# Beta added per block, the mask added through TensorE, wide token comparisons, and values two batches behind the logits

## The chip, the cores and the metric

The kernel runs on one core of a Trainium2 chip. The time is device microseconds (us) of one execution; lower is better. PE is TensorE (matrix multiplications and transpositions), DVE is VectorE, ACT is ScalarE, POOL is GpSimd and SP is SyncE, which here only starts transfers. Each engine works through its own list of instructions in order, and semaphores tie the lists together.

## The reference

The input x has 8 batches of 256 rows of 256 numbers; each batch has a context of 77 rows. The reference computes, cut to what matters:

```
x = x + xattn(layernorm(x), ctx, ctx, mask, gamma, beta)
x = x + ffn(layernorm(x), w_gate, w_gate_up, w_down)

xattn: logits = q k^T / 16; logits = -9e15 where mask == 0; attn = softmax(logits)
       h = attn v;  return layernorm_no_affine(h) * gamma + beta
ffn:   probs = softmax(x w_gate) over 8 experts; keep the top 2, divided by their sum
       g, u = x w_gate_up[e];  y_e = (silu(g) * u) w_down[e];  return sum_e probs_e y_e
```

A constant beta is thus part of x after the first line: it goes into the second layer norm, into the gate and into the output.

## The kernel before

The 2048 rows are 16 tiles of 128 rows, two for each batch. The work has four parts.

**Attention loop.** For each batch b, PE transposes x (`turn_x`, L1122), multiplies with the transposed context (`logits`, L1135), transposes the probabilities (`turn_probs`, L1144) and multiplies them with the context rows (`values`, L1160). The context is transposed and put through the gate once for every two batches (`turn_ctx` L1102, `gate_ctx` L1111). PE's loop of round i does `turn_probs(i-1)`, `turn_x(i+1)`, `logits(i)`, a context step, `values(i-1)`. Many small matmuls (`spin`, L1091) are put in ahead of operations so that PE's clock stays up. DVE takes the statistics of x (`x_stats`, L600 to L605), the masked logits with their minimum (`masked_logits`, L617, of the negated logits, with `cap` from the mask), and the scaled values (`scaled_values`, L643). ACT copies the transposed tiles out of PSUM, takes exponents (L938) and squares (L954). POOL turns the mask into `cap` (`caps`, L450), takes powers (`x_rstd` L455, `scales` L467), adds beta to x (`add_beta`, L461) and adds the scaled values (`x1`, L474). SP then writes the rows to `rows_d`, where experts will gather them, and to the output.

**Routing.** Rows are given slots, expert by expert. `choose` (L654 to L662, DVE) finds each row's two experts, in four groups of tiles (4, 4, 6, 2: `GROUPS`). `ranks` (L1173, PE) counts ranks. `slots` (L669 to L682, DVE) makes a slot number and splits it by integer operations into place (low seven bits) and block (high bits). For each tile and each of the two choices there is then a 128x128 one-hot table of places (`place_sel`) and one of blocks times row number (`token_sel`); PE multiplies the pairs (`tokens`, L1186) and so gets a list of rows for each block. `token_sel` is made by DVE, one instruction of 128 columns for each tile and choice (L695, in `select`); `place_sel` by ACT for the first 11 tiles (`BY_ACT`; Abs at L991 for each column block, then a wide Relu at L995) and by DVE for the others (L693). Part of what DVE does for routing stands in the attention loop.

**First block.** The list gives `gather_0`; POOL starts the gather of block 0 (`gather`, L528); DVE takes the row statistics (`row_stats`, L702 to L717); PE transposes (`turn_tok`, L1255) and starts on the gate and up projections (`gate_up`, L1271).

**Experts.** 39 blocks of 128 gathered rows run in a software pipeline: PE does `gate_up` of a block, the transposition of the activations (`turn_act`, L1281) and `down` of the block before (L1291, L1293), with weights split in high and low parts (`split_high` ACT L344, `split_low` DVE L351; the loads are 512 KB pieces through three buffers, a piece starting only when the low part of the piece three before it is done). The result is weighted in two steps, `low_result` (ACT, L1049, the low half of PSUM times the share) and `weighted` (DVE, L831, the high half times the share plus the former), and POOL adds it to the output with an indirect transfer (`add`, L543). POOL's order for each block b is `gather(b+2)`, `add(b-1)`, `row_scale(b+2)`.

## Time and profile before

| what | value |
|---|---|
| median of 3 runs | 469.33 us (467.65 to 470.09) |
| the profiled execution, its own time | 468.22 us |
| its span, first to last instruction | 466.3 us |
| mean granted TensorE clock | 0.964 of full |
| busy: PE, DVE, ACT, POOL | 431.9, 298.0, 225.3, 178.1 us |

The attention loop runs from about 9 to 54 us of the span, routing to about 72 us, the experts' matmuls start at 78 us, are in their steady rhythm from about 98 us and end at 454 us. Each row below says at which microsecond of the span an instruction starts and how long it takes; in square brackets is the idle time of the engine just before it and what ended it.

### The profile page before, as it was taken

How to read it: one execution, taken by the hardware profiler on the slowest of the kernel's cores; microseconds unless marked ns; L12 is line 12 of the kernel's file. 1: busy time of each engine (PE TensorE's matmuls, PEld its weight loads, DVE VectorE, ACT ScalarE, POOL GpSimd, SP SyncE). 2: the span in 40 equal slices, each digit the busy share in tenths (PEclk: the TensorE clock that was granted, in tenths of full speed). 3: DMA queues.
4: the chain of work that ended last, by engine and by line, in shares of the span. 5: the costliest groups of instructions: out<-in, count | busy, mean ns of one | idle time of the engine just before them, and what ended most of it. 6: DMA issues, size and time to landing. Idle time of an engine off the chain costs nothing.

```text
span 466.3 us, 10417 instructions
## 1 busy us (share of the span) xinstructions
PE 431.9 (93%) x2305; PEld 351.0 (75%) x2306; DVE 298.0 (64%) x780; ACT 225.3 (48%) x476; POOL 178.1 (38%) x177
## 2 busy tenths in 40 slices
PE   7688677899999999999999999999999999999980
PEld 4577344778888888888888888888888888888870
DVE  2748898686578457766775457766765477745430
ACT  3485671545465346635644346635643366434330
POOL 5399702233344224423343224423343234422211
PEclk9798778999999999999999999999999999999996
DMA  7633723245255414543542114542542134211121
GB/s 179 224 115 139 230 90 102 71 118 166 69 117 131 114 23 113 124 124 68 146 126 33 34 23 112 126 124 68 141 131 42 25 71 109 34 34 23 13 23 11
DMA packets 29216, 43.90 MB, mean 94 GB/s; under 512 B 3399, under 2 KB 22832, under 8 KB 29200
## 3 DMA queue, kind: packets, MB, share of 16 engines
q1 hardware_dynamic: 19842, 31.94, 22.1%
q0 software_dynamic: 7520, 10.39, 13.6%
q10 hardware_dynamic: 1838, 1.39, 1.2%
q8 instruction: 6, 0.10, 0.1%
q14 instruction: 10, 0.08, 0.1%
HBM read 34.07 MB, written 9.64 MB: 94 GB/s over the span
## 4 chain that ended last, share of the span: by engine, by line
PE 80%; DVE 7%; DMA 3%; POOL 3%; issue 2%; ACT 1%; DVEq 1%; POOLq 0%; ACTq 0%
PE bank L1271 45%; PE bank L1291 15%; PE bank L1293 8%; PE bank L1281 7%; DMA vals<-in_ctx 2%; PE bank L1255 2%; DVE token_sel L695 1%; PE bank L1091 1%; DVE w L351 1%; POOL x_sb L461 1%; DMA out<-y_sb,out_i 1%; POOL att_scale L467 1%; PE bank L1135 1%; DMA tok<-rows_d,gather 1%; POOL x_sb L474 1%
## 5 line engine op out<-in xcount | busy, mean ns | idle before, releaser
L1271 PE MATMUL bank<-w,tokT_hi 128*128 (+1 forms) x624 | 174.2, 401 | 3.0 <-DVE tokT_lo L807 2.1
L543 POOL DMA_INDIRECT out<-y_sb,out_i x39 | 61.7, 1582 | 227.5 <-DVE y_sb L831 227.5
L1271 PEld LDWEIGHTS bank<-w,tokT_hi 128*128 128x128 f32 x624 | 112.9, 190 | 27.2 <-issue 4.9
L1025 ACT ACTIVATE gated<-bank,row_rstd 128x512 f32<-128x512 f32 x78 | 53.6, 688 | 144.0 <-PE bank L1271 144.0
L1291 PE MATMUL bank<-w,aT_hi 128*128 (+1 forms) x312 | 119.5, 418 | 1.0 <-DVE y_sb L831 1.0
L816 DVE SCALAR_TENSOR_TENSOR act<-bank,row_rstd,gated 128x512 f32<-128x512 f32 x78 | 58.5, 749 | 90.3 <-ACT gated L1025 90.3
L1271 PE MATMUL bank<-w,tokT_lo 128*128 (+1 forms) x312 | 97.3, 393 | 0.0
L1293 PE MATMUL bank<-w,aT_lo 128*128 (+1 forms) x312 | 87.6, 281 | 0.0
L1271 PEld LDWEIGHTS bank<-w,tokT_lo 128*128 128x128 f32 x312 | 58.8, 189 | 13.1
L1291 PEld LDWEIGHTS bank<-w,aT_hi 128*128 128x128 f32 x312 | 58.7, 188 | 11.6 <-issue 1.2
L351 DVE TENSOR_TENSOR w<-raw,w (+1 forms) x48 | 58.7, 1262 | 5.9 <-issue 5.8
L1293 PEld LDWEIGHTS bank<-w,aT_lo 128*128 128x128 f32 x312 | 59.1, 189 | 0.0
L822 DVE TENSOR_TENSOR aT_lo<-bank,aT_hi 128x512 fp32r<-128x512 f32 x78 | 53.1, 681 | 0.0
L528 POOL DMA_INDIRECT tok<-rows_d,gather_i x38 | 48.3, 1270 | 9.5 <-issue 6.9
L344 ACT ACTIVATE w<-raw (+1 forms) x48 | 48.4, 1051 | 0.7 <-issue 0.5
L1281 PE MATMUL bank<-ident,act 128*128 128x128 f32 x312 | 46.8, 272 | 0.4 <-DVE act L816 0.4
L1281 PEld LDWEIGHTS bank<-ident,act 128*128 128x128 f32 x312 | 38.8, 141 | 10.8 <-DVE act L816 0.8
L1032 ACT ACTIVATE aT_hi<-bank 128x512 fp32r<-128x512 f32 x78 | 45.9, 589 | 0.3 <-PE bank L1281 0.3
L1091 PE MATMUL bank<-ones 128*128 128x512 bf16 x89 | 31.9, 455 | 13.6 <-ACT vals L912 5.2
L1049 ACT ACTIVATE y_low<-bank,share_at 128x256 f32<-128x256 f32 x39 | 18.5, 475 | 31.3 <-issue 26.7
L536 POOL TENSOR_TENSOR row_rstd<-row_var,neg_half 128x1 f32<-128x1 f32 x39 | 29.5, 757 | 10.8 <-DVE row_var L715 10.8
L831 DVE SCALAR_TENSOR_TENSOR y_sb<-bank,share_at,y_low 128x256 f32<-128x256 f32 x39 | 18.9, 484 | 19.0 <-ACT y_low L1049 15.7
(151 smaller groups left out, 372.6 us busy)
## 6 DMA issues: line engine op xcount, KB each, us to landing
raw<-in_L_ffn_w_gate_up SPq DMA_DIRECT2D x32, 512.0 KB
raw<-in_L_ffn_w_down SPq DMA_DIRECT2D x16, 512.0 KB
rows_d<-x_sb SPq DMA_DIRECT2D x8, 264.0 KB, 2.1
x_sb<-in_x SPq DMA_DIRECT2D x8, 256.0 KB, 8.3
out<-x_sb SPq DMA_DIRECT2D x8, 256.0 KB, 2.6
out<-y_sb,out_i POOLq DMA_INDIRECT x39
tok<-rows_d,gather_i POOLq DMA_INDIRECT x38, 4.2
vals<-in_ctx ACTq DMA_DIRECT2D x1, 462.0 KB
```

Source lines behind the costliest of these rows:

```text
L344: eng.activation(w2[:, bass.ds(c % (2 * PIECES), 1), :, 0, :].rearrange("p a g d -> p (a g) d"), raw[:, bass.ds(c % RAW, 1)].rearrange("p ...
L351: eng.tensor_tensor(piece[:, :, :, 1, :].rearrange("p a g d -> p (a g) d"), raw[:, bass.ds(c % RAW, 1)].rearrange("p a g d -> p (a g) d"), ...
L528: pool.indirect_dma_start(out=tok[:, b % 2, :], out_offset=None, in_=rows_d, in_offset=bass.IndirectOffsetOnAxis(ap=at, axis=0)).then_inc( ...
L543: pool.indirect_dma_start(out=out, out_offset=bass.IndirectOffsetOnAxis(ap=out_i[:, b:b + 1], axis=0), in_=y_sb[:, b % 2, :], in_offset=No ...
L816: dve.scalar_tensor_tensor(out=act[:, h, :], in0=ps_u[h][:, :], scalar=row_rstd[:, s:s + 1], in1=gated[:, h, :], op0=ALU.mult, op1=ALU.mul ...
L822: dve.tensor_tensor(aT_lo[:, h], ps_aT[h][:, :].rearrange("p (k c) -> p k c", k=CH), aT_hi[:, h].bitcast(F32), ALU.subtract).then_inc(aT_l ...
L1025: act_e.activation(gated[:, h, :], ps_g[h][:, :], ACT.Silu, scale=row_rstd[:, s:s + 1]).then_inc(gated_set, 1)
L1032: act_e.activation(aT_hi[:, h], ps_aT[h][:, :].rearrange("p (k c) -> p k c", k=CH), ACT.Copy).then_inc(aT_hi_set, 1)
L1271: ins = pe.matmul(ps[:, :], tokens_[:, s, k, :], w.rearrange("p a g d -> p (a g) d"), start=(k == 0 and tokens_ is tokT_hi and part == 0), ...
L1281: ins = pe.transpose(ps_aT[h][:, c * P:(c + 1) * P], act[:, h, c * P:(c + 1) * P], ident[:])
L1291: pe.matmul(ps_y[:, :], aT_hi[:, h, c, :], w.rearrange("p a t d -> p (a t d)"), start=(h == 0 and c == 0), stop=False, skip_group_check=True)
L1293: ins = pe.matmul(ps_y[:, 0:D], aT_lo[:, h, c, :], w[:, :, 0, :].rearrange("p a d -> p (a d)"), start=False, stop=(h == 1 and c == CH - 1) ...
```

## The change

- **Beta.** x rows are stored without beta. `add_beta` leaves the attention loop. In the experts' part POOL adds beta to each gathered block (128x256) after its gather has landed, ahead of `add(b-1)`; for block 0 DVE does it at the head of `row_stats`. So that the output has its beta, ACT makes share times beta for each block (`share_beta`, 128x256), and `y_low` becomes a DVE instruction (low half times share plus `share_beta`) at the head of `weighted`; ACT's `low_result` is gone. The two shares of a row sum to one.
- **Mask.** DVE makes `ban` (bf16: 0, or -2^119 where masked) in two instructions (308 and 924 columns). PE adds it into the logits by one more matmul with a bf16 identity for each tile. `masked_logits` becomes one maximum over both tiles, the gate's addition and a small product with rstd; ACT's exponent reads PSUM with rstd as its scale. POOL's four `caps` are gone.
- **Slots and tables.** The slot is split in f32 by adding and removing a large constant. `token_sel` is one DVE comparison for a whole group (4 tiles: 1024 columns), of values without the row number; the row number goes into `place_sel`. ACT makes `place_sel` for 12 tiles, Relu by tile with the number as its scale; DVE makes it for the last 4 (12 to 15), two instructions each.
- **Order.** PE's round i is now `turn_x(i+2)`, `values(i-2)`, a context step, `logits(i+1)`, `turn_probs(i)`; ACT's and DVE's rounds follow. Ten rounds instead of nine. The last two values go to banks 0 and 1 and wait for no scaled values. On ACT's queue the second context load and the second mask load are started ahead of the first compute instruction. `select` of group 0 stands inside the loop. The order around block 0 changes: ACT packs the list ahead of `tok_high(0)` and splits pieces 4 and 5 later; DVE makes the block table ahead of `row_stats(0)`, splits piece 4 after `tok_low(1)`, and has `row_stats(1)` ahead of `gate_half(0, 0, 0)`.

```diff
-    BY_ACT = NT - 5
+    BY_ACT = NT - 4
+    MASKED = -2.0 ** 119
+    ROUND = 1.5 * 2.0 ** 30
...
-        ps_att = [bank[i][:, 0:VAL] for i in (4, 5, 6)]
+        ps_att = [bank[i][:, 0:VAL] for i in (4, 5, 6) * 4 + (4, 5, 0, 1)]
...
-            caps(0)
-            x_rstd(0)
-            caps(1)
-            x_rstd(1)
-            pool.wait_ge(beta_in, 16)
-            add_beta(0)
+            for i in range(B // 2 - 1):
+                x_rstd(i)
             scales(0)
...
-            for b in range(2, B):
-                add_beta(b)
+            x_rstd(B // 2 - 1)
+            for b in range(1, B):
                 scales(b)
                 x1(b - 1)
...
+            def add_beta(b):
+
+                pool.wait_ge(beta_in, 16)
+                pool.wait_ge(tok_in[b % 2], arrival(b, b % 2))
+                pool.tensor_tensor(tok[:, b % 2, 0:D], tok[:, b % 2, 0:D], beta_b[:], ALU.add).then_inc(tok_beta, 1)
...
             for b in range(1, NBLK):
                 if b + 2 < NBLK:
                     gather(b + 2, gather_i[:, b + 2:b + 3])
+                    add_beta(b + 2)
                 add(b - 1)
...
+            def bans(i, b0, b1):
+
+                dve.wait_ge(mask_in[i], 16)
+                part = slice(TPB * b0, TPB * b1)
+                dve.tensor_scalar(ban[:, part, :], cap[:, part, :].bitcast(I32), 0.0, MASKED, ALU.is_equal, ALU.mult).then_inc(ban_set, 1)
...
-                for j in range(TPB):
-                    t = TPB * b + j
-                    dve.tensor_tensor_reduce(out=probs[:, b % 2, j, :], in0=ps_logit[b % 2][:, j, 0:T], in1=cap[:, t, :],
-                                             scale=rstd[:, t:t + 1], scalar=-LOWEST, op0=ALU.add, op1=ALU.min,
-                                             accum_out=neg_max[:, t:t + 1]).then_inc(masked, 1)
+                dve.tensor_reduce(most[:, tiles(b)], ps_logit[b % 2][:, :, 0:T], X, ALU.max).then_inc(most_set, 1)
...
+                dve.scalar_tensor_tensor(out=neg_max[:, tiles(b)], in0=most[:, tiles(b)], scalar=-1.0, in1=rstd[:, tiles(b)],
+                                         op0=ALU.mult, op1=ALU.mult).then_inc(masked, 1)
...
+                dve.tensor_tensor(token_sel[:, 2 * g[0]:2 * (g[-1] + 1), :].rearrange("p (n c) q -> p n c q", c=2),
+                                  count_hi[:].unsqueeze(1).unsqueeze(1).to_broadcast([P, n, 2, P]),
+                                  hi[:, part, :].unsqueeze(3).to_broadcast([P, n, 2, P]), ALU.is_equal).then_inc(token_set, 1)
...
             def weighted(b, s):
 
+                dve.wait_ge(share_beta_set, b + 1)
+                dve.wait_ge(down_done, 2 * b + 2)
+                if later(b, 1):
+                    dve.wait_ge(y_set, b)
+                dve.scalar_tensor_tensor(out=y_low[:], in0=ps_y[:, D:2 * D], scalar=share_at[:, s:s + 1], in1=share_beta[:, s, :],
+                                         op0=ALU.mult, op1=ALU.add).then_inc(y_low_set, 1)
...
+                act_e.activation(share_beta[:, s, :], beta_b[:], ACT.Copy, scale=share_at[:, s:s + 1]).then_inc(share_beta_set, 1)
...
+                    ins = pe.matmul(ps_logit[b % 2][:, j, 0:T], ident_b[:], ban[:, TPB * b + j, :], start=False, stop=True,
+                                    skip_group_check=True)
...
+            for i in range(B + 2):
+                g = i // 2 + 1
+                if i + 2 < B:
+                    turn_x(i + 2)
+                if i >= 2:
+                    values(i - 2)
+                if g < PAIRS and i % 2 == 0:
+                    turn_ctx(g)
+                if i + 1 < B:
+                    logits(i + 1)
+                if g < PAIRS and i % 2 == 1:
+                    gate_ctx(g)
+                if i < B:
+                    turn_probs(i)
```

## Rows read from the trace of the kernel before

**Rows 1.** The page: busy time of the engines, and the group of `low_result`.

```profile
PE 431.9 (93%) x2305; PEld 351.0 (75%) x2306; DVE 298.0 (64%) x780; ACT 225.3 (48%) x476; POOL 178.1 (38%) x177
...
L1049 ACT ACTIVATE y_low<-bank,share_at 128x256 f32<-128x256 f32 x39 | 18.5, 475 | 31.3 <-issue 26.7
```

**Rows 2.** Busy time of each engine by stretch of the span, with granted clock.

```profile
20.00:40.00 20.00, 18.31 (x136) 15.18 (x136) 12.51 (x45) 16.02 (x51) 17.26 (x16) 1.00 0.39 128
...
200.00:300.00 100.00, 99.45 (x523) 83.22 (x522) 63.23 (x146) 49.07 (x95) 35.05 (x31) 1.00 0.36 87
```

**Rows 3.** Timeline of POOL in the attention loop.

```profile
25.50 1.27 POOL L461 TENSOR_TENSOR x_sb<-x_sb,beta_b 128x512 f32<-128x512 f32 x1
26.93 0.71 POOL L467 TENSOR_TENSOR att_scale<-att_var,neg_half 128x2 f32<-128x2 f32 x1 [0.16 <-ACT tok L954]
27.61 1.31 POOL L474 TENSOR_TENSOR x_sb<-scaled,x_sb 128x528 f32<-128x528 f32 x1
...
35.76 1.69 POOL L467 TENSOR_TENSOR att_scale<-att_var,neg_half 128x2 f32<-128x2 f32 x1
```

**Rows 4.** Timeline of PE: two transpositions of probabilities, one round apart.

```profile
26.18 0.38 PE L1144 MATMUL bank<-ident,probs 128*77 128x128 f32 x2
...
29.96 0.38 PE L1144 MATMUL bank<-ident,probs 128*77 128x128 f32 x2
```

**Rows 5.** Timeline of DVE: second context sum, masked logits of batches 0 and 7, last scaled values.

```profile
11.39 1.75 DVE L590 TENSOR_REDUCE ctx_sum<-vals 77x6 f32<-77x1536 f32 x1 [1.81 <-DMA vals<-in_ctx]
15.30 0.29 DVE L617 CUSTOM_DVE_ANT_0 probs<-bank,cap,rstd 128x77 f32<-128x77 f32 x1
...
47.81 0.30 DVE L617 CUSTOM_DVE_ANT_0 probs<-bank,cap,rstd 128x77 f32<-128x77 f32 x1 [1.22 <-PE bank L1135]
...
50.59 0.89 DVE L643 SCALAR_TENSOR_TENSOR scaled<-bank,att_scale,gamma_b 128x264 f32<-128x264 f32 x2 [0.59 <-POOL att_scale L467]
```

**Rows 6.** Timeline of DVE: a wide instruction, then routing.

```profile
29.25 1.22 DVE L351 TENSOR_TENSOR w<-raw,w 128x1024 fp32r<-128x1024 f32 x1
...
51.93 1.09 DVE L674 SCALAR_TENSOR_TENSOR slot_i<-both,last_slot 128x4 int32<-128x4 f32 x1
...
53.82 4.51 DVE L695 TENSOR_SCALAR token_sel<-count_to,parts,number 128x128 f16<-128x128 f16 x16 [0.16 <-DVE parts L682]
...
67.17 0.26 DVE L693 TENSOR_SCALAR place_sel<-count_to,parts 128x128 f16<-128x128 f16 x1
...
71.04 0.16 DVE L782 TENSOR_SCALAR count_up<-bank 128x8 int32<-128x8 f32 x1
```

**Rows 7.** Timeline of ACT in routing.

```profile
53.76 4.78 ACT L991 ACTIVATE place_sel<-count_to,parts 128x128 f16<-128x128 f16 x16 [1.26 <-DVEq L685]
58.57 1.91 ACT L995 ACTIVATE place_sel<-place_sel 128x2048 f16<-128x2048 f16 x1
...
64.53 0.84 ACT L995 ACTIVATE place_sel<-place_sel 128x768 f16<-128x768 f16 x1
```

**Rows 8.** Timeline of DVE and PE at block 0.

```profile
75.39 0.43 DVE L702 BATCH_NORM_STATS2 row_stat<-tok 128x6 f32<-128x256 f32 x1 [0.27 <-DMA tok<-rows_d,gather]
...
78.03 2.06 PE L1271 MATMUL bank<-w,tokT_hi 128*128 128x512 f32 x4 [1.08 <-DVE tokT_lo L807]
```

**Rows 9.** Timeline of DVE and PE in block 1.

```profile
92.55 2.36 DVE L351 TENSOR_TENSOR w<-raw,w  x2 [1.69 <-issue]
...
95.63 0.66 PE L1281 MATMUL bank<-ident,act 128*128 128x128 f32 x4 [0.37 <-DVE act L816]
```

**Rows 10.** Steady experts: timeline around one gather, and landing times from 98 to 449 us.

```profile
235.44 1.45 POOL L528 DMA_INDIRECT tok<-rows_d,gather_i  x1 [0.18 <-issue]
...
241.69 0.48 DVE L831 SCALAR_TENSOR_TENSOR y_sb<-bank,share_at,y_low 128x256 f32<-128x256 f32 x1 [0.40 <-ACT y_low L1049]
...
242.51 0.43 DVE L702 BATCH_NORM_STATS2 row_stat<-tok 128x6 f32<-128x256 f32 x1 [0.34 <-issue]
...
245.89 0.38 PE L1255 MATMUL bank<-ident,tok 128*128 128x128 f32 x2
...
DMA to landing us min/median/max: 2.7/4.5/5.3
```

More of the change, by code:

```diff
@@ L113, in build @@
         probs = sb("probs", [P, 2, TPB, T])
+        most = sb("most", [P, NT])
         neg_max = sb("neg_max", [P, NT])
@@ L183, in build @@
         y_low = sb("y_low", [P, D])
+        share_beta = sb("share_beta", [P, 2, D])
         silu_ready = sb("silu_ready", [P, 1])
@@ L681, in slots @@
                 after(route)
-                step(route, dve.tensor_copy(parts[:, :, part, :], parts_i[:, :, part, :]))
-                if 1 <= i < 3:
-                    after(route)
-                    dve.sem_inc(parts_set, 1)
+                dve.scalar_tensor_tensor(out=neg_lo[:, part, :], in0=hi[:, part, :], scalar=-ROUND, in1=slot[:, part, :],
+                                         op0=ALU.add, op1=ALU.subtract).then_inc(parts_set, 1)
             def select(g):
+                n, part = len(g), span(g)
@@ L990, in places @@
                     for c in range(2):
-                        act_e.activation(place_sel[:, 2 * t + c, :], count_to[:], ACT.Abs, bias=parts[:, 0, t, c:c + 1], scale=-1.0
+                        act_e.activation(place_sel(t)[:, c, :], neg_count[:], ACT.Abs, bias=neg_lo[:, t, c:c + 1], scale=-1.0
                                          ).then_inc(apart_set, 1)
-                part = place_sel[:, 2 * g[0]:2 * (g[-1] + 1), :]
-                act_e.wait_ge(apart_set, 2 * (g[-1] + 1))
-                act_e.activation(part, part, ACT.Relu, bias=1.0, scale=-1.0).then_inc(place_set, 1)
-            places(0, range(0, GROUPS[1][-1] + 1))
-            split_high(act_e, RAW)
-            places(1, range(GROUPS[2][0], BY_ACT))
-            for c in range(GU, PIECES):
-                split_high(act_e, c)
+                for t in g:
+                    part = place_sel(t)
+                    act_e.wait_ge(apart_set, 2 * (t + 1))
+                    act_e.activation(part, part, ACT.Relu, bias=number[:, t:t + 1], scale=neg_number[:, t:t + 1]).then_inc(place_set, 1)
+            places(0, GROUPS[0])
+            places(1, GROUPS[1])
+            places(2, range(GROUPS[2][0], BY_ACT))
             act_e.activation(silu_ready[:], neg_half[:, 0:1], ACT.Silu)
+            split_high(act_e, 3)
             act_e.wait_ge(packed_zero, 1)
```

304 lines of the change are left out of this document (147 added, 157 removed).

## The prediction

> **What bounds the kernel now.** I read the page first: PE is busy 93% of the span and no other engine over 64% [rows 1]. That is an average over unlike stages, so next came the busy time by stretch. From 200 to 300 us PE works 99.45 of 100 us [rows 2]: whatever DVE, ACT or POOL gain or lose in the experts costs nothing until it makes PE wait. From 20 to 40 us POOL is busy 17.3, PE 18.3 and ACT 16.0 of 20 us: three engines are nearly full, and a gain on one meets the next soon. The timelines and the chain of waits then show the stages:
>
> - Start and attention loop. DVE sums the large context load when it has landed, at 11.39, and only then come the first masked logits, at 15.30; those of batch 7 stand at 47.81 and the scaled values of batch 6 at 50.59 to 51.48 [rows 5]. That is (47.81 - 15.30) / 7 = 4.64 us a batch. In it POOL pays beta 1.27, power 0.71 and addition 1.31 [rows 3], and its power takes 1.69 at 35.76. PE's round is 29.96 - 26.18 = 3.78 us with no gap [rows 4].
> - Routing. From 51.48 to 71.04 DVE works without a pause that counts; the list needs its last table [rows 6].
> - First block: the gathered rows are read at 75.39 and PE starts at 78.03 [rows 8].
> - Then PE is the bound to the end.
>
> So the change can pay only ahead of 78 us, and can lose anywhere.
>
> **Attention loop, part by part.** POOL loses eight beta additions (1.27 each) and the mask's work; what stays is 0.71 + 1.31 = 2.0 us a batch, so POOL is no bound. DVE takes over the mask: by the wide row, 1.22 us for 1024 columns [rows 6], 924 columns cost about 1.1 and 308 about 0.5. Nothing in the trace has this form (int32 in, bf16 out); half and double that price are the ends, 0.8 and 3.2 for both. PE adds 16 bf16 matmuls of 77 columns. No row has one; the two 128-column transpositions of rows 4 together take 0.38 including their drain, so I take 0.1 each, with ends of 0 and 0.25. A full round is then 3.78 + 0.2 = 4.0 us on PE.
>
> *Start.* In the old order the masked logits of batch 0 wait on DVE behind the sum of six contexts (1.75) and a second set of statistics. In the new one they stand behind a sum of two and the small mask part, and the load is asked for earlier. I take 12.7 for 15.3. The ends are 11.5 (load no matter) and 15.3 (both early loads delay the x rows by as much).
>
> *Rounds.* Round 0 ends when the first exponents are done, 12.7 + 0.9 = 13.6. Round 1 needs the second mask part, which DVE makes behind the sum of four contexts: 17.5. Rounds 2 to 5 are full ones at 4.0: 33.6. Rounds 6 and 7 have no x to turn, but DVE chooses experts in them: I take 3.2 each, an estimate between half of a full round and a full one, so 40.0. Then the values of batch 6 (about 1.3), a square (0.5) and the power (0.71 plus a hop, 0.8) give 42.6. DVE is still at the first wide comparison, to 43.2, and ends the scaled values 0.9 later, at **44.1 against 51.5: a gain of 7.3**. If the rounds keep the old 4.64 from round 2 on, the end is 3.9 later (4 x 0.64 + 2 x 0.64); if the start gives nothing either, 6.5 later: gain 0.8. The other end is 1.2 earlier plus cheap bans, a gain of 9.
>
> **Routing.** Old, from the scaled values' end: 71.04 - 51.48 = 19.6 us on DVE. New: slots(1) 1.05 (six small steps where there were eight), select(1) 1.22, choose 1.9, last gates and scaled values 1.2, slots(2) 1.1, choose 1.1, the last addition 0.6, select(2) of 1536 columns 1.8, slots(3) 1.0, places 4 x 0.23 = 0.9, select(3) 0.7, places 0.9: 13.4. **Gain 6.2**; most is select, where 16 narrow instructions of 0.28 (4.51 [rows 6]) become two of 1.22, one of them inside the loop, and 20 such steps behind the last slots (from 67.17) become one wide one and eight narrow, select(2) going ahead of them. The wide comparison (f32 in, f16 out) has no row; its ends are 1.0 and 2.0 us for each 1024 columns: -0.8 or +2.4 on the sum.
>
> What is next late is ACT. It makes places for 12 tiles: two Abs of 0.30 (4.78 / 16) and one Relu of 256 columns. From 1.91 for 2048 and 0.84 for 768 columns [rows 7] the Relu is 0.84 ns a column and 0.2 fixed, 0.4 us, or 0.35 when pipelined: 0.95 a tile, 11.4 us in all. ACT begins about where the old one did against the scaled values, 1 us after them, and ends at 12.4, just ahead of DVE's 13.4. But PE holds tokens(1), which needs eight tiles (8.6), ahead of ranks(3), and slots(3) on DVE (due at 9.8) needs that. So the cover is about 1 us; gone, each us of ACT costs one.
>
> One rule speaks against my sum. At 51.93 a small DVE instruction with two inputs takes 1.09 us [rows 6] while POOL is in an addition, and the power at 35.76 takes 1.69 instead of 0.71 [rows 3]. The Trainium skill (SBUF — State Buffer, section Who interferes with whom) says that a DVE instruction with two SBUF inputs and a GpSimd instruction that reads SBUF exclude each other for the whole instruction; these rows agree. By that rule the wide comparisons of groups 0 and 1, which now have two SBUF inputs, can each wait out one `x1` of POOL, and the gain would be some 2.6 us less. My range has that in it.
>
> **First block and ramp.** DVE adds beta to block 0 on the path: by the 1.27 for 512 columns on POOL at most 0.7, by the wide DVE row (1.22 for 1024) 0.4; with a hop **+0.45**. The block table leaves the spot ahead of `tok_low(0)` and two index steps enter: **-0.1**. In block 0 DVE now splits piece 4 behind `tok_low(1)` (1.2); part of it meets idle time, but in block 1 the split at 92.55 already runs so late that PE waits 0.37 at 95.63 [rows 9]: **+0.8**, with ends 0 and 3 (piece 7's load may start only when piece 4 is split, and a late load would hold ACT).
>
> **Steady experts.** For each block ACT gives up 0.475 [rows 1] and takes share_beta, about 0.4; DVE takes 0.48 more, in 9.4 us of which a third is idle [rows 2]. POOL adds beta, about 0.65 (half of 1.27). All this lies beside PE. What could break the cover is the new wait: behind `add_beta` on POOL are the indirect addition and the row power, and DVE's row statistics wait for it. The gather starts at 235.44, lands 2.7 to 5.3 us later (median 4.5), and the statistics start at 242.51, 7.07 after it [rows 10]. Even 5.3 + 0.65 + 0.1 = 6.05 is inside; PE needs the result for 245.89, and the statistics take 1.3 of these 3.4 us, which is 2 us more cover. y_low on DVE instead of ACT takes the same 0.48, but now behind `act_low`: 0.15 later, with the last block alone paying. **+0.15**.
>
> **The sum.** -7.3 - 6.2 + 0.45 - 0.1 + 0.8 + 0.15 = -12.2. The profiled execution took 468.22 us: 456.0. The median of the runs is 469.33, 1.1 above it: 457.1 in their terms, which I give as 457.
>
> **The rivals.**
>
> 1. *The loop hardly gains.* ACT's or DVE's queue, each in order and with more rounds in flight, sets 4.64 again, and the early loads only trade places. For it: three engines over 80% busy [rows 2]. Against: POOL is the fullest without a gap from its beta on, and PE's own round is 3.78. Only 0.8 to 3 of the 7.3 come: -6 or so, 463.
> 2. *ACT's places bound routing.* If a tile costs 1.2 instead of 0.95, ACT ends 3 us later and slots(3) waits: -9, 460.
> 3. *The gather's new wait stalls PE, and the kernel is slower.* Place: `add_beta` on POOL, then row statistics, then `turn_tok`. It decides when landing plus beta exceeds 7.07 + 2 = 9.1 us after the start of the gather. At 9.6 it costs 0.5 us in each of 37 blocks, 18.5: 469.3 - 12.2 + 18.5 = 475.6. Against: 6.05 is the worst that the rows give.
> 4. *No change.* The wide comparison takes 2.0 and more, the loop gains nothing, and the ramp takes 3: about 468.
>
> **Chances.** Forecast (453 to 461.5, with rival 2 inside it at 0.12): 0.70. Rival 1: 0.18. Rival 3: 0.06. Rival 4: 0.06. A measurement of this kernel tells about 0.5% (2.3 us) from no change. Faster: 0.70 + 0.17 = 0.87, same 0.06, slower 0.07. The range takes in the forecast and most of rival 1: 452.5 to 464.5.
>
> **What would show it.** Right: scaled values of batch 6 end near 44 and PE's full rounds take 4.0 to 4.3; `token_sel` is four instructions, the 1024-column ones near 1.2; `count_up` starts near 57.5; PE's first `gate_up` near 65; in the experts POOL's beta addition is about 0.65 and ends over 1 us ahead of the statistics, and PE stays above 99% busy. Wrong: DVE's row statistics waiting on POOL with PE idle at `turn_tok`; `ranks` of the last group waiting on ACT's places; PE at half clock through the loop; the masks' load landing late, so that logits of batch 2 wait for `ban`; or a hole around blocks 0 and 1, with ACT held by piece 7.

## The result: slower, and the profile after

The changed kernel takes 472.45 us (median of 5 runs, 472.24 to 473.82) against 469.33 (467.65 to 470.09): ratio 1.0094, with a 95% interval of 1.0070 to 1.0117. The quotient of the two medians alone is 1.0066. Either way the kernel is slower, by about 1% and by less than 2%; ratios below are those on record. The forecast was 457, so sign and range are both wrong. The profiled execution of the changed kernel has a span of 470.3 us, that of the kernel before 466.3; the stages below are cut from these two.

| stage (us of span) | before | forecast | after | after, three orders mended |
|---|---|---|---|---|
| to the first masked logits or maxima | 15.30 | 12.7 | 16.94 | 11.84 |
| loop, to the end of batch 6's scaled values | 36.18 | 31.4 | 41.00 | 35.28 |
| routing, to `count_up` | 19.56 | 13.4 | 14.36 | 14.04 |
| first block, to PE's first `gate_up` | 6.99 | 7.3 | 9.12 | 7.57 |
| ramp, to `gate_up` of block 2 | 19.72 | 20.5 | 19.88 | 19.96 |
| experts, to the end | 368.55 | 368.7 | 369.00 | 369.31 |
| span | 466.3 | 454.1 | 470.3 | 458.0 |

Routing gave 5.2 of the 6.2 us foreseen. The start lost 1.6, the loop 4.8 and the first block 2.1. The last column is the experiment `e6_three` below.

The page of the changed kernel: busy time of the engines, the new beta addition, and the spin matmuls of PE with what they waited for.

```profile
PE 431.9 (92%) x2318; PEld 352.6 (75%) x2319; DVE 310.1 (66%) x770; ACT 225.0 (48%) x488; POOL 189.4 (40%) x206
...
L533 POOL TENSOR_TENSOR tok<-tok,beta_b 128x256 f32<-128x256 f32 x38 | 28.2, 743 | 110.0 <-DMA tok<-rows_d,gather_i 110.0
...
L1106 PE MATMUL bank<-ones 128*128 128x512 bf16 x86 | 30.0, 442 | 14.4 <-DVE scaled L651 7.1
```

PE's busy sum is that of [rows 1] to the tenth, so the kernel did not get slower by more PE work: it waits more. The third row says for whom: of the 14.4 us of waiting ahead of the spin matmuls, half is for DVE's scaled values. Next, the busy time by stretch (us busy of PE, PE's loads, DVE, ACT, POOL, then the granted clock, DMA share, GB/s; the DMA share is the profile's own figure and comes out a little over 1 in places).

```profile
8.00:12.00 4.00, 0.17 (x3) 0.02 (x1) 0.00 (x0) 0.86 (x2) 0.08 (x1) 1.00 0.89 242
12.00:16.00 4.00, 3.58 (x23) 3.58 (x23) 3.07 (x15) 1.10 (x4) 0.73 (x1) 0.62 1.09 382
16.00:20.00 4.00, 4.00 (x22) 3.54 (x21) 2.35 (x6) 2.10 (x5) 0.32 (x1) 0.53 0.21 64
20.00:40.00 20.00, 16.91 (x131) 13.98 (x130) 13.39 (x50) 15.43 (x45) 7.66 (x8) 1.00 0.32 105
200.00:300.00 100.00, 99.46 (x523) 83.31 (x522) 68.45 (x155) 46.60 (x96) 43.55 (x42) 1.00 0.35 84
```

From 20 to 40 us POOL fell from 17.26 to 7.66 us busy, as the change was to do, and PE fell too, from 18.31 to 16.91 [rows 2]: every engine has idle time, PE 15% of the stretch, and yet the loop is slower. Such a stage is not bound by an engine but by a ring of waits. From 8 to 12 us next to nothing works: ACT 0.86 us, PE 0.17, DVE none.

**Start.** DVE's timeline (start, duration, line, operation, in square brackets the idle time and its releaser), then the row of the chain of waits.

```profile
7.45 0.17 DVE L744 SCALAR_TENSOR_TENSOR wg_sb<-bank,w_gate_sb 128x16 f32<-128x16 f32 x1 [2.93 <-PE bank L1214]
12.11 0.18 DVE L748 SCALAR_TENSOR_TENSOR wg_sb<-wg_sb,gamma_c 128x16 f32<-128x16 f32 x1 [4.48 <-DMA beta_c<-in_L_xattn_beta]
...
16.94 0.32 DVE L623 TENSOR_REDUCE most<-bank 128x2 f32<-128x154 f32 x1 [1.70 <-PE bank L1153]
```

```profile
3.69 8.32 DMA beta_c<-in_L_xattn_beta
```

A load of 0.5 KB takes 8.32 us; by then ACT has asked for the large loads of context, mask and gamma (issued from 1.46 to 3.45 us), and `e1_loads` below shows that these are the reason. The median of such small loads is 5.4 us for gamma's and 6.8 for beta's columns, where it was 2.6 and 2.4 before. DVE waits 4.48 us for the last one, PE behind DVE, and PE's granted clock is then 0.62 and 0.53 in the mean of the next two stretches, mostly its lower level (1.2 GHz). The kernel before has the same dip, with PE waiting for the contexts:

```profile
12.00:16.00 4.00, 1.12 (x5) 0.70 (x5) 3.93 (x18) 1.41 (x4) 1.08 (x1) 0.65 1.10 356
16.00:20.00 4.00, 3.49 (x17) 3.23 (x17) 1.66 (x9) 1.43 (x4) 2.46 (x3) 0.50 0.37 135
```

So the clock is no loss against the kernel before; it is a gain that a quicker start can still collect.

**Loop.** One round on DVE, POOL and PE.

```profile
34.46 0.88 DVE L651 SCALAR_TENSOR_TENSOR scaled<-bank,att_scale,gamma_b 128x264 f32<-128x264 f32 x2
37.54 0.32 DVE L623 TENSOR_REDUCE most<-bank 128x2 f32<-128x154 f32 x1 [2.20 <-PE bank L1153]
...
37.89 0.54 DVE L629 SCALAR_TENSOR_TENSOR neg_max<-most,rstd 128x2 f32<-128x2 f32 x1
38.35 1.21 DVE L366 TENSOR_TENSOR w<-raw,w 128x1024 fp32r<-128x1024 f32 x1
39.49 0.88 DVE L651 SCALAR_TENSOR_TENSOR scaled<-bank,att_scale,gamma_b 128x264 f32<-128x264 f32 x2
```

```profile
37.10 1.31 POOL L478 TENSOR_TENSOR x_sb<-scaled,x_sb 128x528 f32<-128x528 f32 x1
41.45 0.71 POOL L472 TENSOR_TENSOR att_scale<-att_var,neg_half 128x2 f32<-128x2 f32 x1 [3.04 <-ACT tok L972]
42.13 1.30 POOL L478 TENSOR_TENSOR x_sb<-scaled,x_sb 128x528 f32<-128x528 f32 x1
```

```profile
40.03 0.39 PE L1106 MATMUL bank<-ones 128*128 128x512 bf16 x1 [0.95 <-DVE scaled L651]
```

The ring can be read off: `x1` on POOL from 37.10 to 38.41 (1.31); `neg_max`, 0.16 us of work (it takes that in the first four batches), ends only with it, and the split behind it brings DVE to 39.49 (1.08); the first of the two scaled values frees PE's bank at 40.03 (0.54); PE's values, ACT's square and the hops bring POOL to its power at 41.45 (1.42); the power to the next `x1` at 42.13 (0.68). The sum is 5.03 us, and around the three rounds in which DVE splits weights the scaled values start at 29.43, 34.46, 39.49 and 44.51, 5.03 apart. The round forecast was 4.0, the old one 4.64. A second way round lies beside this one and is not much shorter: scaled values, PE's logits, the maxima (42.08), `neg_max`, the split, the next scaled values. `e12_half_x1` shows what is left when POOL no longer sets the time: 4.5 to 4.65.

**Routing.** DVE's timeline, and POOL's beside it.

```profile
55.17 1.22 DVE L693 TENSOR_TENSOR token_sel<-count_hi,hi 128x1024 f16<-128x1024 f32 x1
57.05 0.89 DVE L651 SCALAR_TENSOR_TENSOR scaled<-bank,att_scale,gamma_b 128x264 f32<-128x264 f32 x2 [0.65 <-POOL att_scale L472]
...
58.87 2.38 DVE L693 TENSOR_TENSOR token_sel<-count_hi,hi 128x1024 f16<-128x1024 f32 x1
...
68.95 0.17 DVE L677 TENSOR_TENSOR slot_c<-bank,chosen 128x16 f32<-128x16 f32 x1 [0.37 <-PE bank L1193]
...
72.30 0.16 DVE L793 TENSOR_SCALAR count_up<-bank 128x8 int32<-128x8 f32 x1
```

```profile
55.61 1.35 POOL L472 TENSOR_TENSOR att_scale<-att_var,neg_half 128x2 f32<-128x2 f32 x1 [1.07 <-ACT tok L972]
...
58.87 1.29 POOL L478 TENSOR_TENSOR x_sb<-scaled,x_sb 128x528 f32<-128x528 f32 x1
```

The wide comparison costs 1.22 us, as taken. The second starts in the same moment as an `x1` and takes 2.38: it ends 1.09 us after that `x1`, nearly as if it had begun only then. The first in turn stretches POOL's power from 0.71 to 1.35. In the profile of `e6_three` below, the second comparison went first: it took 1.22, but `x1` took 2.37 and DVE's next step waited 1.19 for it. Which of the two goes first does not matter here; the 1.2 us are lost either way.

```profile
48.06 2.37 POOL L478 TENSOR_TENSOR x_sb<-scaled,x_sb 128x528 f32<-128x528 f32 x1
```

```profile
50.47 0.56 DVE L662 TENSOR_TENSOR versus<-x_sb 128x384 f32<-128x384 f32 x1 [1.19 <-POOL x_sb L478]
```

**First block.** DVE, then ACT, then PE.

```profile
76.81 0.42 DVE L711 TENSOR_TENSOR tok<-tok,beta_b 128x256 f32<-128x256 f32 x1 [0.49 <-DMA tok<-rows_d,gather]
77.27 0.43 DVE L713 BATCH_NORM_STATS2 row_stat<-tok 128x6 f32<-128x256 f32 x1
...
80.55 0.25 DVE L869 TENSOR_SCALAR spare_at<-packed,spare_no 128x39 f32<-128x39 f32 x1 [2.04 <-ACT packed L1034]
...
80.95 0.42 DVE L817 TENSOR_TENSOR tokT_lo<-bank,tokT_hi 128x256 fp32r<-128x256 f32 x1
```

```profile
78.25 0.18 ACT L1034 ACTIVATE packed<-bank 128x16 f32 x1 [4.80 <-issue]
78.84 1.68 ACT L1034 ACTIVATE packed<-bank 128x16 f32 x6 [0.41 <-ACT packed L1034]
80.42 0.38 ACT L1038 ACTIVATE tokT_hi<-bank 128x256 fp32r<-128x256 f32 x1
```

```profile
81.42 0.80 PE L1294 MATMUL bank<-w,tokT_hi 128*128 128x512 f32 x1 [2.60 <-DVE tokT_lo L817]
```

From the row statistics to `gate_up` it took 75.39 to 78.03, 2.64 us, before [rows 8]; now 77.27 to 81.42, 4.15 us. The seven packing copies now stand ahead of `tokT_hi` on ACT, and DVE's index steps, which need them, ahead of `tokT_lo`. The first of the copies starts only at 78.25 because ACT first reads seven start values into registers (seven loads at L1029, starting from 74.2 to 77.6 us). The other 0.6 us of this stage's loss lie ahead of the statistics, most of them the beta addition (0.42 and a hop).

**Experts.** One gather with its beta addition on POOL, and the statistics on DVE.

```profile
239.24 1.45 POOL L525 DMA_INDIRECT tok<-rows_d,gather_i  x1 [0.18 <-issue]
244.41 0.72 POOL L533 TENSOR_TENSOR tok<-tok,beta_b 128x256 f32<-128x256 f32 x1 [3.72 <-DMA tok<-rows_d,gather_i]
```

```profile
246.35 0.43 DVE L713 BATCH_NORM_STATS2 row_stat<-tok 128x6 f32<-128x256 f32 x1 [0.33 <-issue]
```

The addition ends at 245.13, 1.2 us ahead of the statistics, which do not wait for it. PE is busy 99.46 of the 100 us from 200 to 300.

### The profile page after: what moved, and what is told of

Same layout as the page of the kernel before. It is cut to its first block, busy times and chain, and to the rows that moved or that the text cites. A ratio compares the mean times of both kernels' runs of the same rounds, so it can differ in the third digit from the quotient of the medians.

```text
span 470.3 us, 10470 instructions
## 1 busy us (share of the span) xinstructions
PE 431.9 (92%) x2318; PEld 352.6 (75%) x2319; DVE 310.1 (66%) x770; ACT 225.0 (48%) x488; POOL 189.4 (40%) x206
## 4 chain that ended last, share of the span: by engine, by line
PE 81%; issue 5%; DVE 5%; POOL 3%; DMA 3%; ACTq 1%; SPq 1%; DVEq 0%; ACT 0%; POOLq 0%
PE bank L1294 46%; PE bank L1314 15%; PE bank L1316 8%; PE bank L1304 7%; DMA beta_c<-in_L_xattn_beta 2%; PE bank L1278 2%; POOL x_sb L478 1%; PE bank L1106 1%; PE bank L1151 1%; POOL att_scale L472 1%; DMA out<-y_sb,out_i 1%; DVE w L366 1%; ACTq L1029 1%; DVE token_sel L693 1%; PE bank L1137 1%
## 5 line engine op out<-in xcount | busy, mean ns | idle before, releaser
L533 POOL TENSOR_TENSOR tok<-tok,beta_b 128x256 f32<-128x256 f32 x38 | 28.2, 743 | 110.0 <-DMA tok<-rows_d,gather_i 110.0
L1314 PEld LDWEIGHTS bank<-w,aT_hi 128*128 128x128 f32 x312 | 58.7, 188 | 12.1 <-issue 1.3
L366 DVE TENSOR_TENSOR w<-raw,w (+1 forms) x48 | 56.8, 1220 | 5.8 <-issue 5.6
L1304 PEld LDWEIGHTS bank<-ident,act 128*128 128x128 f32 x312 | 38.9, 141 | 11.5 <-DVE act L826 1.6
L1106 PE MATMUL bank<-ones 128*128 128x512 bf16 x86 | 30.0, 442 | 14.4 <-DVE scaled L651 7.1
L1106 PEld LDWEIGHTS bank<-ones 128*128 128x128 bf16 x86 | 8.5, 107 | 24.6 <-DVE scaled L651 9.5
```

Source lines behind the costliest of these rows:

```text
L366: eng.tensor_tensor(piece[:, :, :, 1, :].rearrange("p a g d -> p (a g) d"), raw[:, bass.ds(c % RAW, 1)].rearrange("p a g d -> p (a g) d"), ...
L1304: ins = pe.transpose(ps_aT[h][:, c * P:(c + 1) * P], act[:, h, c * P:(c + 1) * P], ident[:])
L1314: pe.matmul(ps_y[:, :], aT_hi[:, h, c, :], w.rearrange("p a t d -> p (a t d)"), start=(h == 0 and c == 0), stop=False, skip_group_check=True)
```

## The experiments

Each ratio is to the kernel before, run on the same chip in the same session; "the changed kernel" is at 1.0094. Times in us from different sessions differ by up to 0.4% for one kernel (the kernel before had medians of 467.68 to 469.47), so the ratios are what to compare. Stages and rounds are from one profiled execution of each run.

### e1_loads: the large loads go back to where they stood

```diff
-            act_e.dma_start(vals[:, 2:B, 1:D + 1], ctx_t[:, 2:B, :])...
...
-            act_e.dma_start(cap[:, 4:NT, :]..., mask_t[:, 2:B, :])...
-            act_e.dma_start(gamma_b[:, 0:D], ...)...
             centre(0)
             centre(1)
+            act_e.dma_start(vals[:, 2:B, 1:D + 1], ctx_t[:, 2:B, :])...
+            act_e.dma_start(cap[:, 4:NT, :]..., mask_t[:, 2:B, :])...
+            act_e.dma_start(gamma_b[:, 0:D], ...)...
...
-            ctx_means(1, 2, 4)
             bans(0, 0, 2)
             x_stats(0)
+            ctx_means(1, 2, 4)
```

> The changed kernel with the second context load, the second mask load and gamma's load started after the first two centring steps again, and DVE's sum of contexts 2 and 3 behind the first statistics. Theory A (the four small column loads on SP's queue land late, at 12.0 us, because the early large loads keep the DMA engines busy): the last column load lands before 8 us, the first maximum of the logits starts at 12 to 13.5 instead of 16.94, and the end comes 3 to 4.5 us earlier: 468 to 469.5 against 472.5. Rival B (the columns are late for another reason, or the x rows only trade places with the contexts): under 1 us. The rounds of the attention loop keep their 5.03 us by both.

467.47 us (465.20 to 469.76), ratio 0.9980 (0.9960 to 1.0000): the early loads cost some 5 us, 1.1% of the kernel. The edit also moves one DVE sum (`ctx_means`, 0.8 us) back behind the statistics; what that alone gives was not measured. The stretch 8:12 and DVE's first maxima in this kernel:

```profile
8.00:12.00 4.00, 3.07 (x31) 2.76 (x30) 3.14 (x17) 1.28 (x4) 1.05 (x1) 1.00 1.09 273
```

```profile
11.54 0.30 DVE L623 TENSOR_REDUCE most<-bank 128x2 f32<-128x154 f32 x1
```

The small columns land in 2.3 to 2.5 us again (medians), which is Theory A. The first maxima are 5.4 us earlier, and the clock stays at 1.00 to 28 us. The execution profiled took 465.20 us, 2.3 less than the median, so the full clock through the start is shown for it and not for the others. The rounds of the loop are still 5.03 (scaled values at 23.53, 28.56, 33.59, 38.61). Start and loop are two separate losses.

### e9_cols_first: the small columns ahead, the large loads still early

```diff
-            load_x(0)
             sp.dma_start(w_gate_sb[:], ...)
...
+            load_x(0)
```

> The changed kernel with one thing moved: SyncE issues the gate matrix and the four column loads of gamma and beta (0.5 KB each) ahead of the load of x of batch 0; the early large loads of ctx and mask stay where the change put them. Theory (it is the small columns that come late, because they are asked for while the large loads are moving): they land before 8 us instead of at 12.0, x of batch 0 about 3 us later than in the changed kernel, and the first maxima start at 13 to 14.5 instead of 16.94; the rounds stay at 5.03, and the time is 2.5 to 4 us below the changed kernel, 468.5 to 470. Rival (the early large loads hold everything, whatever the order of the small ones): the columns or x of batch 0 still land near 12, first maxima at 16 or later, time within 1 us of the changed kernel's 472.4.

474.63 us (472.05 to 475.72), ratio 1.0117 (1.0066 to 1.0168): no gain where 2.5 to 4 us were expected; the theory fell, the rival held. DVE's timeline, and the stretch 8:12:

```profile
9.94 0.18 DVE L748 SCALAR_TENSOR_TENSOR wg_sb<-wg_sb,gamma_c 128x16 f32<-128x16 f32 x1 [2.07 <-DMA beta_c<-in_L_xattn_beta]
...
12.18 0.75 DVE L613 BATCH_NORM_STATS2 stats<-x_sb 128x6 f32<-128x256 f32 x2 [0.96 <-DMA x_sb<-in_x]
```

```profile
8.00:12.00 4.00, 0.00 (x0) 0.00 (x0) 1.24 (x5) 0.00 (x0) 0.30 (x1) 0.77 1.03 339
```

The columns come 2.2 us earlier and x of batch 0 now lands at 12.1 (8.92 us after its issue in the chain of waits). Whatever stands behind is late: the cause is not the order of the small loads but that 1.05 MB of context, mask and gamma (462, 462 and 128 KB) share the DMA engines, some 90% busy from 4 us on, with what the first batch needs. First maxima: 18.52.

### e2_split_first: DVE's split and choice ahead of the next batch's maxima

```diff
+                if 3 <= i < 6:
+                    split_low(dve, i - 3)
+                if i == 6:
+                    choose(GROUPS[0])
                 if i + 1 < B:
                     masked_logits(i + 1)
                 if i < 3:
                     x_stats(i + 1)
-                if 3 <= i < 6:
-                    split_low(dve, i - 3)
-                if i == 6:
-                    choose(GROUPS[0])
```

> The changed kernel with DVE's weight splits and choose of group 0 put ahead of the masked logits of the same round. Theory A (a ring of waits sets the round: scaled values free a bank, PE does the second values, context step and logits, 2.1 us; DVE's maximum and small product, up to 1.5; then the split, 1.2, stands ahead of the next scaled values, 0.5): the split then lies beside PE's part, a round falls from 5.03 to 3.8 to 4.2 us, and five rounds give 4 to 6 us: 467 to 468.5. Rival B (ACT, POOL or the number of batches in flight sets the round): it stays near 5.0 and the time within 1 us of 472.5.

467.96 us (465.68 to 472.29), ratio 0.9981 (0.9957 to 1.0005). Scaled values start at 32.46, 36.35, 40.81, 44.86, 48.75: rounds of 3.9 to 4.5 in place of 5.03 and 5.4. `neg_max` still takes 1.01 to 1.18 us in each of them, but no split stands between the end of `x1` and the scaled values any more.

### e3_logits_first: PE's context and logits ahead of the values

```diff
-                if i >= 2:
-                    values(i - 2)
                 if g < PAIRS and i % 2 == 0:
                     turn_ctx(g)
                 if i + 1 < B:
                     logits(i + 1)
+                if i >= 2:
+                    values(i - 2)
```

> The changed kernel with PE's context step and logits(i+1) ahead of values(i-2), nothing else. Theory A (the ring): the logits no longer wait behind the values that wait for a bank, so DVE gets its maximum about 1.5 us earlier in a round, and the ring loses PE's logits: rounds of 4.0 to 4.4 instead of 5.03, 3 to 5 us in all: 467.5 to 469.5. Rival B (something else sets the round): no change, or slower, since the values come later and with them squares and powers.

470.62 us, ratio 1.0044 (1.0010 to 1.0077): a gain of 0.5%, where the order on DVE gives 1.1%, and less than the 3 to 5 us expected. Rounds 5.6, 4.75, 4.86, 4.0, and `neg_max` takes 0.16 us in all of them: it no longer meets `x1`, and DVE's scaled values wait about 1 us for POOL's power in its place. The maxima come sooner, but the values, which POOL's power waits for, come later: this shortens one way round the ring and lengthens the other.

### e10_negmax: `neg_max` with one tensor operand

```diff
-                dve.scalar_tensor_tensor(out=neg_max[:, tiles(b)], in0=most[:, tiles(b)], scalar=-1.0, in1=rstd[:, tiles(b)], ...)
+                for t in range(TPB * b, TPB * (b + 1)):
+                    ins = dve.tensor_scalar(neg_max[:, t:t + 1], most[:, t:t + 1], rstd[:, t:t + 1], -1.0, ALU.mult, ALU.mult)
```

> The changed kernel with neg_max made by two DVE instructions for one column each (one tensor operand from SBUF, the scale as a per-row scalar) instead of one with two tensor operands from SBUF. Theory: the one instruction takes 1.01 us where it does 0.16 us of work since it waits for POOL's addition x1; two of the new kind take 0.2 to 0.4 together even beside x1, and since neg_max is a link of the ring that sets the round, the round falls from 5.03 to 4.2 to 4.5 us, scaled values of batch 6 end 3 to 4 us earlier against the first maxima, and the time is 469 to 470. Rival (DVE instructions wait for POOL whatever their operands, or the ring isn't what sets the round): neg_max's group still takes about 1 us or the rounds stay at 5.0, time 472 to 473.

476.30 us (472.20 to 476.94, four runs), ratio 1.0142 (1.0080 to 1.0204). The expectation was wrong on the time and on the round: it falls to 4.95, not to 4.2 to 4.5. DVE and POOL of one round:

```profile
41.18 0.33 DVE L630 TENSOR_SCALAR neg_max<-most,rstd 128x1 f32<-128x1 f32 x2
41.43 1.35 DVE L366 TENSOR_TENSOR w<-raw,w 128x1024 fp32r<-128x1024 f32 x1
...
42.71 0.88 DVE L652 SCALAR_TENSOR_TENSOR scaled<-bank,att_scale,gamma_b 128x264 f32<-128x264 f32 x2
```

```profile
40.39 1.31 POOL L478 TENSOR_TENSOR x_sb<-scaled,x_sb 128x528 f32<-128x528 f32 x1
```

`neg_max` no longer waits (0.203 to 0.215 us in all 16), but the split behind it, which also reads two tensors, does: it ends 1.08 us after `x1`'s end at 41.70, and the splits of the rounds before and after, which took 1.82 and 1.83 us, also end 1.08 us after the end of their `x1`. Until this run I had taken the ring for one of PE and DVE alone with `neg_max` as a slow link; it goes through POOL. That the kernel was slower than the changed one lies in the start of this profile: PE had half clock from 12 to 24 us, and the first scaled values start at 32.80 for 29.43. The edit touches nothing before the first maxima, so why the start was slower stays open.

### e12_half_x1: a shorter addition on POOL

```diff
-                pool.tensor_tensor(x_sb[:, tiles(b), :], scaled[:, b % 2], x_sb[:, tiles(b), :], ALU.add)
+                pool.tensor_tensor(x_sb[:, tiles(b), P:], scaled[:, b % 2, :, P:], x_sb[:, tiles(b), P:], ALU.add)
```

> The changed kernel with POOL's addition x1 over the upper 136 of 264 columns only; it leaves out the attention's part of columns 0 to 127 of the result. Theory (a second ring goes through POOL: x1 holds off DVE's next two-operand instruction, neg_max or the split; the split then delays the scaled values, these PE's values, these ACT's square, and that the power and the next x1): with x1 at about 0.67 us instead of 1.31 neither neg_max nor the split waits for it, and the round is what the PE ring leaves without a wait, about 0.35 from PE's logits to neg_max's start, 0.12, 1.15 for the split: 4.65 to 4.75 us instead of 5.03, three rounds, 1 us in all. Rival (the ring is PE and DVE alone and takes 5.03 with or without POOL): rounds of 5.0 to 5.05, and neg_max or the split still longer than 0.16 and 1.21 us.

The addition leaves out the attention's part of columns 0 to 127. 470.07 us, ratio 1.0048 (1.0025 to 1.0072), by the ratios 2.2 us below the changed kernel. Rounds of 4.47, 4.65 and 4.49. DVE and POOL:

```profile
39.46 0.16 DVE L629 SCALAR_TENSOR_TENSOR neg_max<-most,rstd 128x2 f32<-128x2 f32 x1
39.54 1.22 DVE L366 TENSOR_TENSOR w<-raw,w 128x1024 fp32r<-128x1024 f32 x1
40.67 0.88 DVE L651 SCALAR_TENSOR_TENSOR scaled<-bank,att_scale,gamma_b 128x264 f32<-128x264 f32 x2
```

```profile
38.67 0.76 POOL L478 TENSOR_TENSOR x_sb<-scaled,x_sb 128x272 f32<-128x272 f32 x1
```

Here `x1` ends at 39.43, ahead of `neg_max`, and both DVE instructions have their own length; that round is 4.65, PE's and DVE's share alone. In the two others (no context to transpose, so the maxima come sooner) `neg_max` still waits a little, 0.46 us. So of the 1.03 us by which the changed kernel's round exceeds the forecast 4.0, at least 0.4 to 0.55 are the wait for POOL's addition, on an engine that is busy 38% of that stretch, and the rest is the second way round, with the split between the maxima and the scaled values.

### e4_pack and e5_block0_order: the first block

`e4_pack` moves `tok_high(0, 0)` on ACT and `tok_low(0, 0)` on DVE back ahead of the packing and the index steps:

```diff
+            tok_high(0, 0)
             for e in range(1, E):
                 pack(e)
-            tok_high(0, 0)
```

> The changed kernel with ACT's copy of the turned rows of block 0 and DVE's low part ahead of the packing of the list again, as in the kernel before. Theory A (ACT's reading of seven start values, which ends at 78.25, and then seven packing steps, 2.2 us, stand in front of block 0's transposed rows): PE's first gate_up starts 1.6 to 2.4 us earlier against the start of the gather, and the time falls by 1.5 to 2.3: 470 to 471. Rival B (the later gather list of block 1 takes it back: its rows then come later, as in the kernel before): PE's first gate_up is earlier but block 1 starts later, under 0.7 us in all.

473.52 us (471.82 to 474.28), ratio 1.0108 (1.0071 to 1.0145): no gain. Statistics to `gate_up` fell from 4.15 to 2.48 us, as expected of the cause, but the next transposition of rows then waited 1.65 us for DVE and the `gate_up` behind it 0.74; `count_up` to `gate_up` of block 2 took 29.35 us against 29.00. The rival held: an early first block runs into a late second one.

`e5_block0_order` also puts `block_experts`, the splits of pieces 4 and 5 (DVE's and ACT's) and `gate_half(0)` back where the kernel before had them (DVE's part shown):

```diff
-            block_experts()
             split_low(dve, 3)
+            split_low(dve, 4)
             row_stats(0, 0, 0)
+            block_experts()
...
-            row_stats(1, 1, expert_of(1))
             gate_half(0, 0, 0)
+            row_stats(1, 1, expert_of(1))
```

> The changed kernel with the whole order around block 0 put back: ACT copies the turned rows before it packs, DVE does two splits before the first row statistics and the block table after them, and row statistics of block 1 after the first half of the activations; ACT's splits 3 to 5 stand ahead of the packing. Theory A (packing in front costs 1.7 at the first gate_up, and e4 lost it again because the statistics of block 1, which wait for a late gather, stood ahead of the activations): from count_up to the first gate_up of block 2 it takes 27 to 27.7 us instead of 29.0, time 1.3 to 2 us below the changed kernel's: 470.5 to 471. Rival B (ACT's three splits after the place tables now delay the packing, or PE's clock falls in the wait): no gain.

471.39 us, ratio 1.0051 (1.0030 to 1.0072). `count_up` to `gate_up` 7.57 us, and to that of block 2 27.79 against 29.00 (26.71 in the kernel before). So the loss was in the order of the whole stretch, not in the packing alone.

### e7_beta_only and e8_wide_only: each idea without the rest

`e7_beta_only` is the kernel before with beta added for each block and through `share_beta`; `e8_wide_only` the kernel before with wide `token_sel` comparisons and the row number moved into the place tables. Neither has the new orders.

```diff
-                add_beta(b)
...
                     gather(b + 2, gather_i[:, b + 2:b + 3])
+                    add_beta(b + 2)
...
-                        dve.tensor_scalar(token_sel[:, 2 * t + c, :], count_to[:], parts[:, 1, t, c:c + 1], number[:, t:t + 1], ...)
+                dve.tensor_tensor(token_sel[...n tiles...], count_f[:]..., parts[:, 1, part, :]..., ALU.is_equal)
```

> The kernel before with only the beta part of the change: stored rows have no beta, POOL adds it to each gathered block, DVE to block 0, ACT makes share times beta, DVE makes y_low. Theory A (hidden beside PE in the experts; in the loop POOL was nearly full, so it gains some there): loop 2 to 4 us shorter, first block 0.45 later, experts equal within 0.5: 466 to 468. Rival B (the gather's new wait on POOL or DVE's extra 0.48 makes PE wait in the experts): 470 or more. Rival C (the loop is bound by the others too): within 1 us of before.

468.43 us, ratio 0.9993 (0.9968 to 1.0019). The loop gains 2.7 us (14.57 to 48.09), the first blocks give back 1.0 and the experts took 1.5 more than in the profile of before (PE busy 99.05 of the 100 us from 200 to 300, for 99.45). With that nothing is left that can be measured, as rival C had it for the total, although the loop did gain.

> The kernel before with only the wide comparisons: token_sel by one comparison for a group, the row number in the place tables, slots as before with integers, DVE still makes the places of the last 5 tiles. Theory A (16 narrow instructions of 0.28 become two of 1.22, and 20 later steps become one wide one and ten narrow): count_up 3.5 to 5 us earlier, 464.5 to 466. Rival B (ACT's Relu by tile takes more than the one wide Relu and bounds): 1 to 2 us only.

467.62 us, ratio 0.9960 (0.9940 to 0.9981): faster by 0.4%, less than expected. Routing took 17.3 us for 19.56, a gain of 2.3 where 3.5 to 5 were expected. The first two comparisons took 3.41 us together, for 2 x 1.22, one of them beside an addition on POOL, and PE waited 1.17 us for ACT's places, so both the exclusion between DVE and POOL and rival 2 of the prediction show here a little.

### e6_three: the change with three orders mended

`e1_loads`, `e2_split_first` and `e5_block0_order` together; no arithmetic differs from the changed kernel.

> The changed kernel with three repairs: the loads of e1, the split ahead of the masked logits of e2, the order around block 0 of e5. Theory A (three separate losses that add up: 5.3 and 5.3 by the runs of e1 and e2, about 1.5 by e5): 12 us below the changed kernel, about 460 to 461, ratio to the kernel before 0.981 to 0.985. Rival B (the gains of e1 and e2 are largely one, the clock of PE in the first 25 us): 464 to 466.

459.46 us (459.10 to 459.93), ratio 0.9793 (0.9756 to 0.9830): faster than both kernels, and 3.0% below the changed kernel, where the gains of `e1_loads`, `e2_split_first` and `e5_block0_order` (1.1, 1.1 and 0.4%) add up to 2.7%. Its DVE timeline:

```profile
11.84 0.30 DVE L623 TENSOR_REDUCE most<-bank 128x2 f32<-128x154 f32 x1
...
26.44 1.01 DVE L629 SCALAR_TENSOR_TENSOR neg_max<-most,rstd 128x2 f32<-128x2 f32 x1
27.37 0.88 DVE L651 SCALAR_TENSOR_TENSOR scaled<-bank,att_scale,gamma_b 128x264 f32<-128x264 f32 x2
```

The stages are in the table above. `neg_max` still waits for `x1` here, and the ring without the split, with the terms read in the changed kernel, 1.31 + 0.54 + 1.42 + 0.68 = 3.95 us, is close to the 3.88 and 3.89 of two of its rounds; the others take 4.05 and 4.47. A part of the gain is PE's clock: PE does the same matmuls in 426.3 us busy where both other kernels need 431.9, and the granted clock is 1.00 from 12 to 20 us, where the kernel before has 0.65 and 0.50.

### e11_all: the same with both small edits

`e6_three` with `e9_cols_first` and `e10_negmax`.

> The changed kernel with five edits together: the three of the version that took 459.46 (large loads again after the centring, choices ahead of the next batch's maxima on DVE, the order of before around block 0), the columns of gamma and beta ahead of x of batch 0, and neg_max by two single-operand instructions. If columns and neg_max still cost there: first maxima near 11.8 or up to 0.5 later (x of batch 0 is asked for later), rounds of 3.9 as before because PE sets them, and 0 to 1 us less in all: 458.5 to 459.5. Rival (both are off the path once the order is mended): within 0.5 us of 459.46, or 1 to 2 us more if x of batch 0 becomes the last to land.

461.56 us (457.49 to 463.65), ratio 0.9871 (0.9815 to 0.9927), slower than expected. The profiled execution is the fastest of all, span 455.7, with a loop of 33.56 us against 35.28 and rounds of 3.2 to 4.5: off the ring of the split, `neg_max` does pay. But the four runs spread over 6 us, and the median is no better than that of `e6_three`. What spreads them stays open, so that one remains the best version shown.

## Why the prediction was wrong, step by step

- **Start, 12.7 for 15.3: wrong, it was 16.94.** The bound named for it ("both early loads delay the x rows by as much", 15.3) was the right mechanism and too small: not the x rows alone but every load behind is late. `e1_loads` shows it, `e9_cols_first` that putting the small loads first does not mend it. The other half of the reasoning, DVE's shorter way to the maxima, held: with the loads late they come at 11.54, the lower bound of 11.5.
- **"Rounds 2 to 5 are full ones at 4.0": the step that failed.** I took PE's own work of a round, 3.78 + 0.2, for the round, and the overlap of DVE's split and POOL's addition with it for complete. The same rows gave 4.64 as the mean of the old rounds, so 3.78 was already less than a round there. PE's work was as said (a mask matmul shows as 0.20 us and adds 0.03 to 0.05 to the chain, where 0.1 was taken; `ban` is 0.31 and 0.63 us, where 0.5 and 1.1 were), but the new order on DVE closes a ring through `neg_max`, the split, the scaled values, PE, ACT and POOL's `x1`: 5.03. With half of `x1` (`e12_half_x1`) it is 4.5 to 4.65, with the split out of the ring (`e2_split_first`) 3.9 to 4.5. The stage was forecast 4.8 us shorter and came out 4.8 longer. Rival 1 said that a queue in order could set the round, but at no more than the old 4.64, so it still came out as a gain; it was argued down by POOL being the fullest engine, where [rows 2] have PE at 18.31 us and POOL at 17.26. I never followed one scaled value round the ring.
- **The rule on DVE and POOL was applied to the wide comparison alone.** Here the second comparison took 2.38 us, so rule and trace agree (the Trainium skill, SBUF — State Buffer, section Who interferes with whom), and that cost 1.2 us, with 0.6 on POOL's power, which falls into the loop's stage. In the loop the same exclusion costs more: `neg_max` ends only with `x1`, or the split starts its work only then (`e10_negmax`, `e12_half_x1`). The trace of before already had splits of 2.20 us in the loop.
- **Routing, -6.2: right in sign and nearly in size, -5.2.** The missing 1.0 is the stretched comparison, 1.16. The 0.28 taken for a narrow instruction held such a wait too: one of the 16 took 1.17 us beside an addition on POOL. In addition, slots(3) waited 0.37 us for PE. ACT's places took 1.12 us a tile (2.43 + 2.06 for four) where 0.95 was taken: rival 2 began to show, hardly more.
- **First block, +0.35: wrong, it was +2.13.** Beta on DVE cost 0.42, as taken. That `pack` goes ahead of `tok_high(0)` on ACT is in the diff and not in my sum: I counted DVE's moved steps and not ACT's; it is 1.5 of the 2.1 us.
- **Ramp +0.8, experts +0.15: +0.16 and +0.45.** The ramp is within its bounds, in part by luck: the wait it named did grow by 0.8 (PE waits 1.17 us ahead of the transposition in block 1, for 0.37), and shorter waits before it made up for most of that. The experts took 0.3 more than said; which wait that is stays open. The wait after the gather (rival 3) is not there, the addition ending 1.2 us ahead.
- **Sum.** +1.6 + 4.8 - 5.2 + 2.1 + 0.2 + 0.5 = +4.0, the difference of the spans. With three orders mended the same arithmetic gains 10 us (469.47 to 459.46); the orders that came with the change cost 13 to 14 (by the medians and by the ratios), more than the ideas bring. "Slower" had a chance of 0.07, nearly all of it for rival 3, which did not happen: the sign was missed by a mechanism that had no rival of its own.

## What to carry to other kernels

When an edit changes the order in several in-order queues, follow one buffer round the whole ring (who frees it, who stands ahead of that on its engine, who must have ended first) and add up; the sum of an engine's work is only a lower bound of the round. A load moved earlier can delay what the first step waits for: here a 0.5 KB column, and, with the columns first, a 256 KB tile. Judge an idea and its order separately: the same arithmetic was 0.9% slower and 2.1% faster.

## What the runs showed of the hardware

- A small f32 DVE instruction of one column, with a per-row scalar, took 0.203 to 0.215 us whatever POOL did (16 of 16); one of two columns with two tensors in SBUF took 0.16 alone and up to 1.18 beside `x1`. The exclusion works the other way too: POOL's power 1.35 us for 0.71 behind a wide comparison, `x1` 2.37 for 1.31. One tensor input is no safe sign, though: in the kernel before, an f16 comparison of 128 columns with per-row scalars took 1.17 us beside an addition on POOL, for a median of 0.31.
- A 0.5 KB load took 8.32 us when large loads were moving; the medians of such loads were 2.4 and 2.6 us in the kernel before.
- ACT reads seven start values into registers ahead of its packing copies. DVE had written them at 74.17, and the first copy began at 78.25. Each read takes 0.27 to 0.48 us, and they start 0.57 us apart on average, so seven values cost ACT about 4 us. In the kernel before the same reads (72.9 to 76.3) lay beside the wait for the gathered rows.
